# Attention context turned to token rows by VectorE in 32x32 blocks, output product in two halves, in a fused mixer layer on one core

## What is computed

```
xn  = layernorm(x)
out = x + attention(xn) + experts(xn)

attention: qkv = xn @ w_qkv + b_qkv, 16 heads of 16 channels
           heads 0..3: causal over the whole sequence; heads 4..15: causal, at most 64 tokens back
           ctx = softmax(q k^T / 4) v ; returns ctx @ w_out + b_out
experts:   8 experts, products of projections with a running sum over tokens,
           weighted by a softmax router, twice (forward and inverse branch), then @ W_O
```

## Time and profile before

| | |
|---|---|
| median of 3 runs | 1515.61 us (1514.74 to 1518.65) |
| the profiled execution | 1516.97 us, of which the span from first to last instruction is 1515.3 us |
| busy: TensorE, VectorE, ScalarE, GpSimd | 1425.3, 882.5, 852.4, 575.5 us |
| granted TensorE clock, mean | 0.996 of full speed |
| chain of work that ended last | TensorE 75%, VectorE 11%, ScalarE 8%, issue 5% |
| a pair of chunks | 179.6 us (`finish` of chunk 3 starts at 443.8 us, that of chunk 5 at 623.3 us) |

### The profile page before, as it was taken

The page is one execution under the profiler, slowest core; times in us unless marked ns, Lnnn a source line. Parts: engine busy times, 40 slices in busy tenths (PEclk is TensorE's granted clock), DMA queues, the critical chain, the costliest instruction groups (busy, mean ns, idle before and its releaser), DMA issues.

```text
span 1515.3 us, 36826 instructions
## 1 busy us (share of the span) xinstructions
PE 1425.3 (94%) x14977; PEld 1072.4 (71%) x14977; DVE 882.5 (58%) x1935; ACT 852.4 (56%) x1512; POOL 575.5 (38%) x663
## 2 busy tenths in 40 slices
PE   5999999999999999999999999999999999999997
PEld 4577775867758686686857777586775868678673
DVE  6676773556645675465755577356664567546451
ACT  3446557474665547565474645647466563756544
POOL 1044351444425343352424435143442524335241
PEclk9999999999999999999999999999999999999999
DMA  9322507253251625317053350615325162531600
GB/s 226 81 77 75 145 23 170 65 121 118 64 144 32 156 82 120 102 39 187 31 141 96 83 144 30 162 60 121 118 73 136 32 165 73 120 102 40 174 30 15
DMA packets 153789, 150.56 MB, mean 99 GB/s; under 512 B 28468, under 2 KB 136885, under 8 KB 153573
## 3 DMA queue, kind: packets, MB, share of 16 engines
q1 hardware_dynamic: 153620, 148.22, 37.7%
HBM read 106.98 MB, written 34.87 MB: 94 GB/s over the span
## 4 chain that ended last, share of the span: by engine, by line
PE 75%; DVE 11%; ACT 8%; issue 5%; POOL 1%; DMA 0%; ACTq 0%; POOLq 0%; DVEq 0%
PE PS L660 35%; PE PS L781 11%; PE PS L815 3%; PE PS L932 3%; PE PS L801 3%; PE PS L901 3%; PE PS L869 3%; PE PS L883 3%; ACT HE L1116 2%; PE PS L913 2%; PE PS L987 2%; PE PS L845 2%; ACT HE L1108 2%; DVE block_peak L1292 2%; DVE PL L1384 1%
## 5 line engine op out<-in xcount | busy, mean ns | idle before, releaser
L1547 POOL TENSOR_TENSOR PL<-prod,PH 128x512 fp32r<-128x512 f32 x128 | 164.7, 1287 | 215.1 <-ACT PH L1078 215.1
L1542 POOL TENSOR_TENSOR prod<-prod,rest 128x512 f32<-128x512 f32 x96 | 123.3, 1287 | 265.1 <-ACT prod L1068 146.0
L660 PE MATMUL PS<-XH,WH 128*128 128x512 f32 x512 | 218.3, 426 | 4.5 <-DVE XL L1232 1.9
L1292 DVE TENSOR_REDUCE block_peak<-PS 128x4 f32<-128x512 f32 x288 | 181.0, 684 | 54.2 <-PE PS L815 54.2
L660 PE MATMUL PS<-XL,WH 128*128 128x512 f32 x512 | 203.7, 398 | 0.0
L660 PE MATMUL PS<-XH,WL 128*128 128x512 f32 x512 | 203.2, 397 | 0.0
L1078 ACT ACTIVATE PH<-prod 128x512 fp32r<-128x512 f32 x128 | 80.8, 631 | 209.6 <-DVE prod L1365 209.5
L1525 POOL TENSOR_SCALAR_AFFINE_SELECT HE<-HE 128x256 f32<-128x256 f32 x128 | 51.0, 411 | 347.9 <-ACT HE L1116 345.3
L1116 ACT ACTIVATE HE<-PS 128x512 f32<-128x512 f32 (+1 forms) x320 | 159.7, 552 | 24.8 <-PE PS L883 22.6
L1068 ACT ACTIVATE prod<-PS 128x512 f32<-128x512 f32 x128 | 76.1, 594 | 125.3 <-PE PS L660 114.9
L1285 DVE TENSOR_REDUCE peak<-PS 128x4 f32<-128x512 f32 x192 | 120.6, 682 | 41.1 <-PE PS L801 41.1
(11 more groups left out here) (196 smaller groups left out, 3142.3 us busy)
## 6 DMA issues: line engine op xcount, KB each, us to landing
parts_d<-area SPq DMA_DIRECT2D x32, 768.0 KB, 5.1
area<-parts_d SPq DMA_DIRECT2D x128, 192.0 KB, 8.4
rest<-weights_d SPq DMA_DIRECT2D x192, 128.0 KB, 2.9
area<-parts_d SPq DMA_DIRECT2D x32, 576.0 KB, 8.4
tok<-in_L_attn_x_dram SPq DMA_DIRECT2D x16, 512.0 KB, 6.3
xt<-in_L_attn_x_dram SPq DMA_DIRECT2D x16, 512.0 KB, 4.2
wide<-weights_d SPq DMA_DIRECT2D x64, 128.0 KB, 3.0
out_dram<-xt SPq DMA_DIRECT2D x16, 512.0 KB, 3.7
```

What stands on the lines that cost most here:

```text
L660: ins = e.matmul(ps, a, b, start=first and k == 0, stop=last and k == n - 1, skip_group_check=True)
L1292: e.tensor_reduce(block_peak[ch % NC][:, t, :, j], psum(i).rearrange("p (a k) -> p a k", a=4), AX_X, ALU.max).then_inc(bank_read[i])
L1542: e.tensor_tensor(prod[:, j % 3, :], prod[:, j % 3, :], wide[j % WIDE], ALU.mult).then_inc(weighed)
L1547: e.tensor_tensor(PL[:, j % 2, :], prod[:, j % 3, :], PH[:, j % 2, :].bitcast(F32), ALU.subtract).then_inc(plo)
```

## The change

The TensorE transposes of the context go, and so do the ScalarE copies ahead of them.

- `ctx` takes the place of `cin` and `cout`. VectorE transposes the PSUM tile in 32x32 blocks to `craw[:, 1]`. Each block of 32 tokens is turned in its place, so partition 32g + t holds head g of token t of the block, and column 32b + d channel d of block b. Then reciprocal of the 16 sums and multiplication into `ctok[:, k]`, 16 of each 32 columns. Two groups share one `ctok[:, k]`: 1 and 2 the first (k = 0), 3 and 0 the second (`CTX_AT`). Group 2 now uses bank 4, where it used bank 7.
- `cturn` transposes `ctok[:, k]` back in 32x32 blocks with VectorE, and ScalarE copies the high part to PH. `crest` is the VectorE subtraction for PL. They take the place of `cparts`. The half k = 0 is made ready right after the local attention, ahead of `keep` and of `hidden` 0 to 3; its `crest` comes after `hidden` 3. The half k = 1 is in the tail.
- `finish` is two products of 12 matmuls: that of k = 0 is the last of the pieces woven into the global attention, that of k = 1 comes after the first three `lpeak` of the next chunk.
- The channels stand in another order: row 32g + 16 half + d of half k. The rows of `w_out` are loaded in the same order (16 DMAs for one), and those of `b_qkv` for the values too (5 for one).

```diff
+    CTX_AT = {1: (0, 0), 2: (0, 1), 3: (1, 0), 0: (1, 1)}
+
+    def ctx_bank(grp):
+        return 7 if grp % 2 else 4
...
@@ the plan
     def add_lav(ch, grp, half):
-        add("lav", ch, grp, half, uses=["bank7"] if half == 0 else [])
+        add("lav", ch, grp, half, uses=[f"bank{ctx_bank(grp)}"] if half == 0 else [])
...
         if half == 1:
-            add("cin", ch, grp)
+            add_ctx(ch, grp)
...
-            if n > 2 and half:
-                order[-1].append((add_cout, ch, grp - 1))
...
         run(experts[0] + peaks[0])
+        if ch:
+            add_finish(ch - 1, 1)
         weave(experts[1:split], peaks[1:])
...
         add_lav(ch, NL // 4, 1)
+        add("cturn", ch, 0)
         if nxt:
             add("keep", ch + 1)
             add("stacks", ch + 1, "local")
-            add_hidden(ch + 1, 0)
-            add_hidden(ch + 1, 1)
-        add_cout(ch, NL // 4)
-        if nxt:
-            add_hidden(ch + 1, 2)
-            add_hidden(ch + 1, 3)
+            for j in range(2 * DB):
+                add_hidden(ch + 1, j)
+        add("crest", ch, 0)
...
+        side.append([(add_finish, ch, 0)])
         weave(order, side)
...
-        add_cout(ch, 0)
...
-        for k in range(DB):
-            add_on("cparts", ch, k, uses=[score_use()])
+        add("cturn", ch, 1)
...
-        add_finish(ch)
+        add("crest", ch, 1)
+    add_finish(CHUNKS - 1, 1)
@@ TensorE
-                elif kind == "cout":
-                    ch, grp = key
-                    r, cb, tb = grp % 2, 7 if grp else 4, 4
-                    q.wait_ge(bank_read[cb], use("bank7", "lav", ch, grp, 0) if grp else use("bank4", "gav", ch, 0, 0))
-                    take(tb, *stage)
+                elif kind == "finish":
+                    ch, k = key
+                    q.wait_ge(ctx_lo, nth("crest", ch, k))
                     for t in range(T):
-                        ins = e.transpose(psum(tb, lo=t * P, hi=(t + 1) * P), craw[:, r, t * P:(t + 1) * P], ident[:, :])
...
@@ ScalarE
-                elif kind == "cparts":
+                elif kind == "cturn":
                     ch, k = key
-                    q.wait_ge(ctx_turned, DB * ch + k + 1)
+                    q.wait_ge(ctx_turned, nth(*stage))
                     q.wait_ge(phl_read[k], use(f"phl{k}", "mix", ch, 6 + k, 1))
-                    e.activation(PH[:, k, :], psum(where[stage][0]), ACT.Copy).then_inc(ctx_hi)
+                    e.activation(PH[:, k, :], cturned, ACT.Copy).then_inc(ctx_hi)
...
@@ VectorE
+                elif kind == "ctx":
                     ch, grp = key
...
+                    e.transpose(craw[:, 1, :], psum(cb)).then_inc(bank_read[cb])
+                    q.wait_ge(bank_read[cb], use(f"bank{cb}", *(("lav", ch, grp, 0) if grp else ("gav", ch, 0, 0))))
+                    q.step(e.reciprocal(cinv[:, :], raw_t[:, :, HD]))
+                    q.wait_step()
+                    q.step(e.tensor_tensor(ctok[:, k, :].rearrange("p (b e) -> p b e", e=32)[:, :, half * HD:(half + 1) * HD], raw_t[:, :, 0:HD],
+                                           cinv[:, :].unsqueeze(2).to_broadcast([P, C // 32, HD]), ALU.mult))
...
+                elif kind == "cturn":
                     ch, k = key
...
+                    q.wait_step()
+                    e.transpose(cturned, ctok[:, k, :]).then_inc(ctx_turned)
+
+                elif kind == "crest":
+                    ch, k = key
+                    q.wait_ge(ctx_hi, nth(*stage))
+                    e.tensor_tensor(PL[:, k, :], cturned, PH[:, k, :].bitcast(F32), ALU.subtract).then_inc(ctx_lo)
```

More of the change, by code:

```diff
@@ L1365, in vector_program @@
                     e.tensor_tensor(prod[:, r, :], psum(3), prod[:, r, :], ALU.mult).then_inc(bank_read[3])
-                elif kind == "cout":
+                elif kind == "ctx":
                     ch, grp = key
-                    r, tb = grp % 2, 4
-                    raw_t = psum(tb).rearrange("p (t g e) -> p t g e", t=T, g=4)
-                    q.wait_ge(craw_read[r], use(f"craw{r}", *stage))
+                    k, half = CTX_AT[grp]
+                    cb = ctx_bank(grp)
+                    raw_t = craw[:, 1, :].rearrange("p (b e) -> p b e", e=32)
+                    if grp:
+                        q.wait_ge(*av_read(*[s for s in plan.stages if s[0] == "lscore" and s[1:3] == (ch, grp)][-1]))
+                    else:
+                        q.wait_ge(*av_read(*last_global(ch)))
@@ L1579, in sync_program @@
                             load(dst[:, b, :].rearrange("p (k r) -> p k r", k=KE), src[:, b * P:(b + 1) * P, :].rearrange("k p r -> p k r"), 2)
-                    load(rOUT, w_out.rearrange("(b p) d -> p b d", p=P), 3)
+                    for grp in range(NH // 4):
+                        k, half = CTX_AT[grp]
+                        for g in range(4):
+                            row = 32 * g + HD * half
+                            load(rOUT[row:row + HD, k, :], w_out[HD * (4 * grp + g):HD * (4 * grp + g + 1), :], 3)
                     for dst, src in zip(rU, (U_fwd, U_inv)):
@@ L1680, in sync_program @@
                         e.dma_start(wide[j % WIDE][R * k:R * (k + 1), :], weights_d[2 * j + k:2 * j + k + 1, :].to_broadcast([R, C])).then_inc(wide_in[j % WIDE], 16)
-                elif kind == "finish":
-                    ch, = key
+                elif kind == "finish" and key[1] == 1:
+                    ch, k = key
                     q.wait_ge(bank_read[1], use("bank1", "open", ch))
```

83 lines of the change are left out of this document (31 added, 52 removed).

## The result

The changed kernel takes 1602.2 us (median of four runs, 1601.0 to 1604.2), the kernel before in the same series 1515.4 us. The ratio is 1.057, with a 95% interval of 1.055 to 1.059. The forecast was 1566 us with a range of 1532 to 1592: the direction was right, the loss was 87 us in place of 50, and the time lies outside the range.

The account below looks back on a forecast made before the run. TensorE, busy 94%, was taken as the bound, now held up by VectorE's path to the Gelus: 1515.6 plus 32 (net +2.15 us in 15 chunks), 18 (clock) and 0 (ends) gave 1566 us, range 1532 to 1592.

Parts of the forecast that it names:

- The walk of chunk 4: End of local attention: VectorE's parts, copy, table load and Gelu bring `hidden` 2 4.4 us later; net +2.15 us per chunk.
- The shorter and the longer path: Rivals on VectorE's transpositions: little over 311 ns gives 1539 us, chance 0.1; 1.24 us gives 1594 us, chance 0.06.
- a clock that stays up: Rival: TensorE stalls ahead of `hidden` 2 but its clock does not fall, 1548 us; chance 0.2.
- a gain: Rival: TensorE is never held up at `hidden` 2 and only the removed work counts, 1461 us; chance 0.07.
- no change: Half-way case: a stall of 2 us, time within 0.3%; chance 0.05.
- The clock: After the stall, TensorE at half speed for up to 3.4 us: 0 to 1.7 us, taken as 1.2, 15 times, +18 us.
- The tail: Chunk end on TensorE: last `cout`, `cparts` and the wait ahead of `finish` go, splitting costs 0.1; gain 2.25 us per chunk.
- `cparts` gives 1.2: Tail, x(1) to x(2): 2.66 us, where six matmuls with nothing between take about 1.5; removing `cparts` gains 1.2.
- In the tail I find no new wait: Tail: VectorE and ScalarE need 3.7 us to PL of half 1 (5.1 in even chunks), ready before TensorE needs it.
- The ends: Last chunk -1 us, preparation +1 us for 15 more `w_out` loads and 4 of biases; together 0.
- The rule on the table load: Skill page's drain of about 1.38 us beside the 1.28 us load would add some 20 us; the trace's row was used instead.
- The transfers: `keep` moves from 502.02 to 504.54, delaying transfers for `weigh` 0; hidden behind the stall, else one to two us in even chunks.

Follow-up runs that it names:

- the moved copy: Changed kernel with `cturn` of half 0 planned behind the four hidden stages, so ScalarE copies PH after the Gelus: 1499.6 us, 0.989 of before.
- the two runs with three and with two rounds: Changed kernel with the six matmuls of `hidden` 1 issued three or two times more, result overwritten, in chunks after the first: 1571.0 and 1572.0 us.
- the run with little weighing: Changed kernel with GpSimd's weighing of experts' parts 0 to 2 done over 8 of 512 columns, in every chunk but the first: 1603.0 us.
- the run with the scalings moved: Changed kernel with VectorE's four scalings of the next tokens moved behind `crest` of half 1: 1602.2 us, 1.057 of before.

## Why the prediction failed

**The bound and the path: right.** That VectorE, the copy and the Gelu would hold `hidden` 2 back, 15 times, was measured row by row and confirmed by the moved copy. The walk of chunk 4 had `hidden` 2 at 507.26 us, 20.0 behind the `rows` of the global peaks (487.26 in the timeline of before); in the changed kernel these are at 510.16, and `hidden` 2 came at 530.37, 20.2 behind them. The transposition of 128x512 takes 0.71 us, the value taken. The shorter and the longer path are out, and so are a clock that stays up, a gain and no change.

**The stall's size: 5.5 us too small.** In even chunks the stretch grows by 4.6 us (4.4 forecast), in odd ones by 4.9. From VectorE's first key part to `hidden` 2 the walk had 15.0 us, and it is 15.2 in every chunk. The step that the product of `ctx` stays at 0.42 us, with the next instruction 0.34 behind it, is the one that failed here: that of group 2 takes 0.57 us on this path and costs 0.15 more. 34 of the 64 products run beside GpSimd and take 0.90 on average, up to 1.53. Those of group 1 (1.1 to 1.3 us) are off the path: VectorE waits for the first key part behind them. Before, all 64 take 0.42, beside GpSimd or not. They read one input from PSUM then, and `craw` and `cinv` in SBUF now. The step that the key and query parts keep their durations was wrong as well and came out by luck. The cast of the first key part, before and now:

```profile
493.45 0.92 DVE L1259 CAST area<-rest 128x512 bf16<-128x512 f32 x1
```

```profile
515.93 1.50 DVE L1237 CAST area<-rest 128x512 bf16<-128x512 f32 x1
```

It runs beside GpSimd for longer than before, and this part takes 0.9 us more; the casts of the second key part and the first query part no longer meet GpSimd, and each of these parts takes 0.4 us less. Together that is under 0.1. In odd chunks another 0.27 us lies between `mix` and the local rows, ahead of the walk.

**The clock: 18 forecast, 33 measured, the largest miss.** The mechanism was right, and the two runs with three and with two rounds show it. The step that failed is "up to 3.4 us after the stall", with 1.7 us as the most it could cost. The last chunk showed one low stretch of 3.4 us, and I took the length of one instance for the most. After the 4.3 us the low stretch lasts about as long in five of the seven odd chunks, but 6.8 us in the other two and in all even ones, and costs 1.6 and 2.2 to 2.7 us. One instance gave no upper bound. What sets the one or the other length is not settled; in the run with little weighing, and in chunks 1 and 13 here, the longer one came where the tail ahead was some 1 us shorter.

**The tail: -34 forecast, -20 measured.** The step "`cparts` gives 1.2" failed, and it is as large as the whole miss. From x(1) to x(2) it is now 2.33 us against 2.66 in the tails behind even chunks, a gain of 0.33; behind odd ones it was 2.34 before, a gain of nothing. The transposes had filled a wait for bank 2, which ScalarE must first empty. With all of `finish` in the tail, as the run with the halves together has it, the gain is 1.4 us per chunk and not 2.25, without any wait for PL.

The sentence "In the tail I find no new wait" failed a second time at PL of half 1, by 5.6 us in five tails. I had counted 1.4 us for the scalings from a trace in which GpSimd waited for a transfer until 526.07 and so left VectorE alone; now they take 2.4 to 3.4. The stall itself brought the two together, as the run with the copy moved shows. And moving half of `finish` into the global attention was put down at nothing; it costs 0.5 us in even and 2.15 us in odd chunks, 19 us in all, in place of the 1.58 per chunk, 24 us, that it takes from the tail. These two nearly cancel. The other parts of the tail came as forecast: `weight_rows` to x(1) fell by 0.99 us (0.8 forecast), x(2) to its successor by 0.40 (0.35).

**The ends: right in sum.** +0.6 us together, 0 forecast; the last chunk gave nothing where 1 us was forecast, and the preparation cost 0.6 in place of 1. Half 0 made TensorE wait 3.2 us in the last chunk (some 3 forecast).

**The rule on the table load.** The Gelu starts 0.01 us after the end of the load, on the path itself now: 528.34 + 1.28 = 529.62, and 529.63. The Trainium skill, ScalarE: Activation LUTs, section "What ACT_TABLE_LOAD costs", has some 1.38 us more for a switch. The trace does not agree here. The estimate of 20 us worked out from that figure would have brought the sum nearer to the result for a wrong reason.

**The transfers.** Hidden behind the stall, as forecast. Without the stall GpSimd waits for them longer, but no run shows what that costs: with the copy moved alone, `mix` to the local rows takes 9.9 us in odd chunks in place of 9.5 (9.2 before the change), and it takes 9.9 too in the run with the scalings moved, where the stall is still there.

**The range.** Its upper end, 1592, lay just under the longer path at 1594, which had the clock at 1.5 us per chunk. No case held that two of the terms would come out worse together, and that is what happened.

## What to carry to other kernels

A copy that waits for a late producer, placed in the queue of an engine ahead of what frees TensorE's banks, can turn a gain of 1% into a loss of 6%: look at who stands behind each new wait before costing the work that it removes. Work taken out of a place where TensorE waits anyway gives little or nothing back, so read the distance to the next release, not the duration of the instructions. And while there is a stall that lowers the clock, measured gains and losses elsewhere are not to be trusted; remove the stall first, then try the small moves again.

## What the runs showed of the hardware

- **The clock.** In the profiled executions, after a wait of TensorE of 1.5 us ahead of `hidden` 2 the granted clock stays at 2.4 GHz in all chunks; after 2.9 us it falls in 12 of 15; after 4.3 us in every one, to 1.2 GHz for 3.4 or 6.8 us. Filling the wait with matmuls whose result is thrown away gained 31 us.
- **VectorE beside GpSimd.** Four scalings over 128x256 with all operands in SBUF take 1.38 us alone and 2.3 to 4.3 us beside GpSimd's products over 128x512 (1.3 us each). A cast over 128x512 from fp32 to bf16 in SBUF takes 0.43 us alone and 0.8 to 1.5 beside GpSimd. A subtraction over 128x512 with both inputs in SBUF takes 0.69 us alone and 1.37 beside it. Products that read one input from PSUM keep their 0.42 and 0.69 us. The Trainium skill, SBUF — State Buffer, section "Who interferes with whom", says that an instruction of VectorE with two inputs in SBUF contends with one of GpSimd that reads SBUF, and names `tensor_scalar` among those that can take the shared ports. The traces agree, with these numbers; for the scalings and the subtraction the run with little weighing shows it by taking the one side away. Moving an operand from PSUM to SBUF, as this change does, has this price.
- **The transposition** in 32x32 blocks takes 0.71 us for 128x512 in fp32, from PSUM and from SBUF alike: all 96 took 0.69 to 0.72 us, beside GpSimd or not.
